# A selective-scan block: three PSUM banks for the drive and three for the transposed states, six units multiplied on GpSimd, and the interleaved steps at new places

## The reference, cut to what matters

```python
xn = layernorm(x)
x_in, z = split(xn @ W_in + b_in)                  # 256 channels each
xc = silu(causal_conv4(x_in) + conv_b)
Bm, Cm = split(xc @ W_xp + b_xp)                   # 16 states each, per token
delta = softplus(xc @ W_dt + b_dt)
h_t = exp(delta_t * A) * h_{t-1} + (delta_t * xc_t) * B_t    # per channel and state
y_t = sum_over_states(h_t * C_t) + D_skip * xc_t
r = LN(xn + (y * silu(z)) @ W_out + b_out) * alpha + beta
x1 = x + layernorm(r)
out = x1 + layernorm(fp8_fake_quant(layernorm(x1)) @ fp8_fake_quant(W)^T + bias)
```

## Time and profile before

| | us |
|---|---|
| median of 3 runs | 610.04 (608.99 to 610.43) |
| the profiled execution | 609.68 |
| its span, first to last instruction | 607.9 |
| DVE busy | 509.6 (84%) |
| PE busy | 522.5 (86%) |
| ACT busy | 434.2 (71%) |
| POOL busy | 330.5 (54%) |
| mean granted TensorE clock | 0.937 of full |

### The profile page before, as it was taken

One profiled execution on the slowest core, in us unless ns is written; L12 is line 12 of the kernel. 1 busy time (PEld: TensorE's weight loads), 2 busy tenths in 40 slices (PEclk: granted clock), 3 DMA queues, 4 the chain that ended last, 5 costly groups with the idle time before them and its releaser, 6 DMA issues.

```text
span 607.9 us, 10292 instructions
## 1 busy us (share of the span) xinstructions
PE 522.5 (86%) x2879; PEld 400.3 (66%) x2879; DVE 509.6 (84%) x1023; ACT 434.2 (71%) x875; POOL 330.5 (54%) x329
## 2 busy tenths in 40 slices
PE   7998999997999888998999789998999779666193
PEld 4566787876787756777787657776777568556030
DVE  5367799888889979898889879898989999977786
ACT  3569884988498956988398938896698857730264
POOL 3054365567374846657456828565665857520054
PEclk8999999999899999998999999989999999888555
DMA  7103351145304350245013530535035603550018
GB/s 203 40 1 70 71 105 36 36 82 101 62 13 92 75 102 1 57 95 113 13 35 69 104 72 1 104 69 104 1 64 96 117 2 65 109 104 1 0 29 196
DMA packets 19921, 41.15 MB, mean 68 GB/s; under 512 B 3744, under 2 KB 10016, under 8 KB 19872
## 3 DMA queue, kind: packets, MB, share of 16 engines
q0 software_dynamic: 9936, 34.87, 30.3%
q1 hardware_dynamic: 9936, 5.78, 3.5%
HBM read 3.68 MB, written 2.10 MB: 10 GB/s over the span
## 4 chain that ended last, share of the span: by engine, by line
PE 38%; DVE 19%; issue 14%; POOL 14%; ACT 8%; DMA 3%; DVEq 1%; POOLq 1%; ACTq 0%
PE drive L1052 12%; PE hT L1068 8%; DVE state L1274 7%; PE fbank L988 5%; DMA acc<-term 3%; DVE acc_d L1297 3%; PE fbank L1006 2%; ACT decay L780 2%; POOL diag L538 2%; POOL u L511 2%; POOL acc L554 2%; POOL acc L565 2%; POOL acc L563 2%; ACT term L801 2%; ACT nrm L691 2%
## 5 line engine op out<-in xcount | busy, mean ns | idle before, releaser
L1274 DVE TENSOR_TENSOR_SCAN state<-decay,drive 128x512 f32<-128x512 f32 x256 | 297.1, 1202 | 23.0 <-PE drive L1052 12.3
L780 ACT ACTIVATE decay<-delta,a_neg 128x510 f32<-128x510 f32 x256 | 170.5, 731 | 46.9 <-DVE state L1274 38.2
L1052 PE MATMUL drive<-diag,uT 128*128 128x256 f32 x768 | 188.5, 390 | 0.8 <-DVE uT L1474 0.8
L1068 PE MATMUL hT<-ident,state 128*128 128x128 f32 x1024 | 147.5, 282 | 31.6 <-DVE acc_d L1297 22.2
L1068 PEld LDWEIGHTS hT<-ident,state 128*128 128x128 f32 x1024 | 119.8, 145 | 64.2 <-issue 25.0
L1052 PEld LDWEIGHTS drive<-diag,uT 128*128 128x128 f32 x768 | 143.2, 197 | 18.2 <-DVE uT L1474 1.0
L801 ACT ACTIVATE term<-hT,Ct 128x256 f32<-128x256 f32 x256 | 102.9, 485 | 4.9 <-PE hT L1068 4.9
L538 POOL TENSOR_SCALAR_AFFINE_SELECT diag<-Bt 128x512 f32<-128x512 f32 x96 | 65.9, 716 | 34.0 <-PE drive L1052 17.4
L1297 DVE SCALAR_TENSOR_TENSOR acc_d<-hT,Ct,acc_d 128x256 f32<-128x256 f32 x160 | 66.6, 471 | 6.3 <-PE hT L1068 6.2
L523 POOL TENSOR_TENSOR scaled<-uT,Bt 128x1024 f32<-128x1024 f32 x32 | 65.6, 2051 | 8.3 <-DVE uT L1474 4.2
L554 POOL DMA_DIRECT2D acc<-term x64 | 60.0, 938 | 7.9 <-ACT term L801 6.4
(11 more groups left out here) (194 smaller groups left out, 667.2 us busy)
## 6 DMA issues: line engine op xcount, KB each, us to landing
acc<-term POOLq DMA_DIRECT2D x64, 512.0 KB, 4.6
out_dram<-x_all SPq DMA_DIRECT2D x7, 256.0 KB, 3.1
x_all<-term POOLq DMA_DIRECT2D x5, 256.0 KB, 3.9
x_all<-in_L_attn_x_dram SPq DMA_DIRECT2D x2, 256.0 KB, 3.7
state<-in_L_attn_conv_w_dram SPq DMA_DIRECT2D x1, 512.0 KB, 5.2
w_in<-in_L_attn_W_in_dram SPq DMA_DIRECT2D x1, 256.0 KB, 3.9
w_dt<-in_L_attn_W_dt_dram SPq DMA_DIRECT2D x1, 256.0 KB, 4.0
out_dram<-x_all SPq DMA_DIRECT2D x2, 128.0 KB, 2.8
```

The costliest lines, as they stand in the source:

```text
L780: last = nc.scalar.activation(decay[:, g % DECAYS, h, :, s, 1:], delta[:, par, h, :, 1:], ACT.Exp, scale=a_neg[:, h, SG * g + s:SG * g + s ...
L1052: last = nc.tensor.matmul(dst[:, :, P * c:P * c + P], uT[:, par, TC * b + c, P * h:P * h + P], diag[:, n % DIAGS, c, :, :], start=True, st ...
L1068: last = nc.tensor.transpose(hT[:, c, DI * s + P * h:DI * s + P * h + P], state[:, n % STATES, h, s, P * c:P * c + P], ident[:, :])
L1274: nc.vector.tensor_tensor_scan(state[:, n % STATES, h, :, :].rearrange("p s t -> p (s t)"), decay[:, g % DECAYS, h, b, :, :].rearrange("p ...
```

## The change

`drive` and `hT` get three banks each. Both are used as rings over halves or chunks in order: with q = 2n + k the bank is q mod 3, starting again at bank 0 in each pair. A write waits for the reader of the same bank's previous content: three places back, or, for the first three of a pair, the last use of that bank in the pair before (q = 30, 31 and 29). Borrowed banks are renamed. `MUL_U` becomes six units, 1, 2, 5, 7, 8 and 13, instead of 2, 6, 10 and 12; the two buffers `scaled` stay. Many places in the four step tables change.

```diff
-MUL_U = (2, 6, 10, 12)
+MUL_U = (1, 2, 5, 7, 8, 13)
+RING = 3
-POOL_STEPS = dict(front_root=(0,), front_residual=(28,), front_u=(25,), back_gate=(9,), back_affine=(18,),
-                  back_sum=(25,), sum_states=(7,), back_root=(13, 22, 27))
-ACT_STEPS = dict(back_h2T=(47,), front_xin=(8, 9), silu_table=(21,), front_silu=(21, 22, 23), exp_table=(23,),
-                 front_norm=(14,), front_xnT=(23,), front_dt=(29, 30), front_exp=(35,), front_log=(37,),
-                 front_uT=(42, 46), back_norms=(32, 40, 45))
-PE_STEPS = dict(front_in=(0, 6, 18, 21), front_transpose=(23,), front_dt=(24, 28), front_bc=(36,),
-                front_ut=(40, 45), back_y=(12, 14), back_out=(18,), back_transpose=(45,))
-DVE_STEPS = dict(front_stats=(1,), front_shift=(4,), front_low=(19,), front_bc=(25,), front_delta=(24,),
-                 back_y=(8, 8), back_norms=(12, 13, 17, 21, 24, 27, 27), back_amax=(31,))
+POOL_STEPS = dict(front_root=(5,), front_residual=(31,), front_u=(25,), back_gate=(8,), back_affine=(18,),
+                  back_sum=(25,), sum_states=(5,), back_root=(15, 22, 27))
+ACT_STEPS = dict(back_h2T=(46,), front_xin=(1, 9), silu_table=(21,), front_silu=(21, 22, 23), exp_table=(23,),
+                 front_norm=(12,), front_xnT=(23,), front_dt=(29, 32), front_exp=(36,), front_log=(36,),
+                 front_uT=(41, 45), back_norms=(31, 40, 44))
+PE_STEPS = dict(front_in=(2, 6, 18, 21), front_transpose=(24,), front_dt=(25, 29), front_bc=(36,),
+                front_ut=(40, 42), back_y=(12, 14), back_out=(18,), back_transpose=(46,))
+DVE_STEPS = dict(front_stats=(2,), front_shift=(3,), front_low=(21,), front_bc=(25,), front_delta=(24,),
+                 back_y=(8, 9), back_norms=(13, 13, 17, 22, 24, 27, 27), back_amax=(31,))
+def ring(n, k):
+    return (2 * n + k) % RING
+def ring_before(n, k):
+    q = 2 * n + k
+    if q >= RING:
+        return 0, (q - RING) // 2, (q - RING) % 2
+    q = max(r for r in range(2 * UNITS) if r % RING == q)
+    return -1, q // 2, q % 2
-        drive = ps("drive", [P, 2, HALVES, SG * L])
-        hT = ps("hT", [P, TC, SG * DI])
+        drive = ps("drive", [P, RING, SG * L])
+        hT = ps("hT", [P, RING, SG * DI])
...
-                old = trailing(pr, par, n, 2)
                 for h in range(HALVES):
-                    if old:
-                        pe.wait_ge(scan_done, nth(old[0], 2 * UNITS, 2 * old[2] + h + 1))
-                    dst = drive[:, n % 2, h, :].rearrange("p (s t) -> p s t", s=SG)
+                    back, old_n, old_h = ring_before(n, h)
+                    if not back or pr.after(1):
+                        pe.wait_ge(scan_done, nth(pr.plus(back), 2 * UNITS, 2 * old_n + old_h + 1))
+                    dst = drive[:, ring(n, h), :].rearrange("p (s t) -> p s t", s=SG)
...
             def transpose_states(pr, par, n, c):
-                old = trailing(pr, par, n, 1)
-                if old:
-                    if old[2] // PAIR in DIRECT:
-                        pe.wait_ge(direct_done, nth(old[0], DIRECTS, directs(turn(DIRECT, old[2]), SG - 1, c)))
-                    else:
-                        pe.wait_ge(term_ready, nth(old[0], TC * SCALED_N, TC * turn(SCALED_G, old[2]) + c + 1))
+                back, old_n, old_c = ring_before(n, c)
+                if not back or pr.after(1):
+                    old_pr = pr.plus(back)
+                    if old_n // PAIR in DIRECT:
+                        pe.wait_ge(direct_done, nth(old_pr, DIRECTS, directs(turn(DIRECT, old_n), SG - 1, old_c)))
+                    else:
+                        pe.wait_ge(term_ready, nth(old_pr, TC * SCALED_N, TC * turn(SCALED_G, old_n) + old_c + 1))
...
```

More of the change, by code:

```diff
@@ L401, in back_bank @@
             if is_last(pr):
-                return (bbank[:, :], fbank[:, :], drive[:, 0, 0, :], drive[:, 0, 1, :])[k]
+                return (bbank[:, :], fbank[:, :], drive[:, 0, :], drive[:, 1, :])[k]
             return bbank[:, :]
@@ L409, in f_bank @@
         def f_bank(g):
-            return drive[:, g // 2 % 2, g % 2, :]
+            return hT[:, 2, :] if g % 4 == 3 else drive[:, g % 4, :]
         def other(grp, par, d):
@@ L800, in scale_c @@
                     into = acc[:, par, b, c, s, :] if j < PAIR else term[:, j % TERMS, c, s, :]
-                    last = nc.scalar.activation(into, hT[:, c, DI * s:DI * s + DI], ACT.Copy,
+                    last = nc.scalar.activation(into, hT[:, ring(n, c), DI * s:DI * s + DI], ACT.Copy,
                                                 scale=Ct[:, par, TC * b + c, SG * g + s:SG * g + s + 1])
@@ L1155, in _ @@
             amax_to_all(fbank, wq_top, wq_max, wq_global)
-            keep_warm(drive[:, 1, 1, :], 4)
+            keep_warm(hT[:, 2, :], 4)
             pe.wait_ge(w_in_loaded, 16)
@@ L1173, in _ @@
             pe.wait_ge(sz_ready, 1)
-            keep_warm(drive[:, 1, 0, :], 16)
+            keep_warm(drive[:, 2, :], 16)
             for h in range(HALVES):
@@ L1190, in _ @@
             last_pair = Pair(PAIRS - 1)
-            keep_warm(drive[:, 1, 1, :], 28)
+            keep_warm(drive[:, 2, :], 28)
             pe.wait_ge(h2T_ready, PAIRS - 1)
@@ L1194, in _ @@
                 back_y(last_pair, 1, h)
-            keep_warm(drive[:, 1, 1, :], 8)
+            keep_warm(drive[:, 2, :], 8)
             pe.wait_ge(e_gated, HALVES)
@@ L1275, in scan_half @@
                                              decay[:, g % DECAYS, h, b, :, :].rearrange("p s t -> p (s t)"),
-                                             drive[:, n % 2, h, :], 0.0, ALU.mult, ALU.add).then_inc(scan_done, 1)
+                                             drive[:, ring(n, h), :], 0.0, ALU.mult, ALU.add).then_inc(scan_done, 1)
             def add_direct(pr, par, n):
@@ L1288, in add_direct @@
                         a = acc_d[:, par, b, c, :]
[L1289 removed]
+                        src = hT[:, ring(n, c), DI * s:DI * s + DI]
                         by = Ct[:, par, TC * b + c, SG * g + s:SG * g + s + 1]
```

11 lines of the change are left out of this document (5 added, 6 removed).

## The result

Median of four executions 614.43 us (611.17 to 615.71), before 609.75 in the same comparison: ratio 1.0061, 95% interval 1.0032 to 1.0089 (the two medians alone give 1.0077). Predicted were 600.8 us.

A forecast was written before the change was run, and what follows sets the result against it. Bound: PE's chain plus ACT's 21 us in each slot's first half, DVE work with waits in the second. From 609.7, +1.6 - 6.6 - 1.9 - 1.5 - 0.8 = -9.2 gives 600.5, median 600.8; range 592 to 612.

The forecast's parts named there:

- rival 1: POOL (GpSimd) multiplies hold DVE instructions, one hold of 1.27 us in each of seven slots: 609.7 us, no change; chance 0.08.
- finish 1 to 3 us before DVE asks: Moved places of `front_low`, exp, log, `front_ut`, norms and roots: each moves at most a scan, finishing early enough; no cost.
- A: First half of a pair's slot, T to unit 8's second scan: 30.9 us at full clock, +1.6 us together over six.
- B: Second half of a slot, unit 8's second scan to the next T: ended waits and cheaper `bshift`, -6.6 us over six.
- last pair: Last slot, without a front: a shorter small DVE instruction and an ended `back_y` wait, -1.5 us.
- clock term: PE at half clock at three of six slot starts instead of two, +5.0 us; bounds 0 and 9.9.
- T: Start of a slot's first scan; `front_in(1)` on PE was worked out to end at T+9.5.
- First pair: Start of the kernel: shorter drives 1 and 5, but `front_stats` falls where DVE works: -0.8 us, bounds -2.5 and +1.5.
- end: Very end, direct sums of units 14 and 15: a third bank ends waits for transposed states, -1.9 us.
- Rival 2: Three drive banks starve DVE in B, each miss costing up to a scan: 15.7 us, 616.5 us in all; chance 0.17.
- worth nothing alone: Six units on POOL save PE 1.7 us a slot, hidden behind ACT in A and DVE in B: no gain.
- the transposed states gain little from a third bank inside the loop: In the loop a stalled pair of chunks ends 0.44 us earlier, on PE, which is not the bound there.

The follow-up runs named there:

- e1_low19: The changed kernel with `front_low` one unit (two scans) earlier, at place 19 instead of 21: 596.16 us, ratio 0.9776.
- e8_before_six: The kernel before the change with six units multiplied on POOL (GpSimd) instead of four, nothing else: 609.78 us, ratio 0.9986.
- e15_add_lag3: e1_low19 with the last two places' accumulating transfers issued ahead of their diagonal or multiply, and transfer lag 3 units instead of 4: 602.72 us, ratio 0.9890.

## Why the prediction was wrong

**The step that failed** is the one that set rival 1 aside: "Against: by my walk they miss each other by 0.3 us or more." They met within 0.07 us, in all six loop slots, and `front_low` was held for 2.55 us in each. `front_low`'s move to 21 stood in the sum at nothing ("finish 1 to 3 us before DVE asks"): its finish was checked, not what POOL does at its new place. The rival's size was wrong as well: 1.27 us a slot, from a small instruction that met the tail of a multiply, where an instruction that meets its start waits out the multiply and the diagonal behind it, 2.55. At that size rival 1 is 600.8 + 15.3 = 616.1, near the 614.43 measured. That nearness is partly luck: of the stretches, A came out 4.2 us lower than forecast, B beside the holds 2.9 and the last pair 1.4, and the edges 2.9 higher.

**Not foreseen**: the two loop edges, +2.9 us. The later transfers were in the prediction, the stretch they would collide with was not, though its list of waits in pair 4's slot of the kernel before could have had the edge at that slot's end, 3.56 us.

**A was right at full clock to 0.1 us, too high with its clock term.** The eight matmuls of `front_in(1)` end at T+9.7 in pair 6's slot (T = 427.19), 0.2 later than worked out:

```profile
433.25 3.60 PE L1003 MATMUL fbank<-xnT,w_tap 128*128 128x512 f32 x8
436.69 0.28 PE L1008 MATMUL fbank<-edge,ident 128*128 128x6 f32 x2
```

A is 30.95 us in pairs 2, 4 and 6 (worked out: 30.9), 30.44 to 31.55 in the others. The +5.0 for half clock at slot starts came to about 1: pair 5's 31.45 against 30.44 in pair 3, the slot behind the other edge; pair 1's 31.55 ran at full clock. Half clock came in B instead, in four of the six, 27 us in all, where e1_low19 has 7: in pair 4's for 6.8 us, after PE had waited 1.93 us for the scan behind the held `front_low`. It cost little but in pair 1's, 33.15 us against 31.80 in pair 5's at full clock:

```profile
336.64 1.13 PE L1067 MATMUL drive<-diag,uT 128*128 128x256 f32 x4 [1.93 <-DVE state L1290]
```

```profile
338.10:344.90 6.80, 6.80 (x34) 6.80 (x34) 6.54 (x10) 5.29 (x13) 5.70 (x5) 0.50 0.40 77
```

**Right in B**: `bshift` 0.16, `bvar` 0.17, the root's 1.16 unchanged, transposes no longer waited for; without the holds B is 1.6 us a slot below before, against 1.1 predicted. The wait at `back_y` is gone, the one at `back_res` only shrank (0.64), and that at unit 8 grew to 1.67 (predicted 1.5).

**First pair, last pair, end**: -0.7, -2.9 and -1.6 against -0.8, -1.5 and -1.9. Of the end's waits one is left (0.43).

**Rival 2** (the ring starves DVE) is real, but the new places and units are its cure: +24 us for the rings alone, against 15.7 as priced, and in A as much as in B. That PE's 1.7 us a slot are "worth nothing alone" came true only as a sum with the hold of `bvar`; beside rings and new places the six units are worth 8.8 us. That "the transposed states gain little from a third bank inside the loop" is in doubt: with two banks for them and the new places DVE waits 14.2 us for them, but no run changes that ring alone.

## What to carry to other kernels

Before moving a DVE instruction, or one on GpSimd, write down what the other of the two does in that very microsecond: a move by one unit cost 18 us here by the medians (15 of it the held instruction itself), more than all the rest of the change won. A sum of zero, as with the six units alone, can hide such a hold too. A held instruction shows no idle time, so look for groups whose mean duration changed, not for waits. And keep transfers clear of a hardware loop's back edge.

## What was not expected of the hardware

- A DVE instruction that meets a GpSimd instruction can have to wait out the next one behind it too: `front_low` ended 0.55 us after the second in both forms measured (3.23 and 1.95 us), and so did `bvar` in e8_before_six, which came 0.89 us after the multiply's start and ended as the diagonal did (1.88). In e15_add_lag3 `front_low` came 0.39 us after an affine's start and ended 0.55 us after that one alone (1.43), though a multiply followed. Why is open; the rows differ in that the diagonal begins 0.3 us before the multiply ends, the multiply of e15 only 0.04 before the affine ends.
- GpSimd pays too: `beta` took 1.60 us where `front_low` ran beside it (e1_low19), 1.28 in the kernel after.
- A loop's back edge costs DVE 2.9 to 3.3 us with idle DMA engines and up to 5.7 with one transfer of 512 KB in flight; two in a row cost no more than one.
